# A decoder layer's cross attention: queries stacked by way of DRAM, keys in one run per row, and new orders for all engines

## What is computed

```python
x = layernorm(x + self_attn(x, W))       # one head, scores x.x/16, softmax; probabilities under 0.01 go to a rank-one term
x = layernorm(x + cross_attn(x, ctx, mask, Wq, Wk, Wv, Wo, biases))   # 16 heads of 16
x = layernorm(x + moe(x, Wr, Wi, Wo))    # 8 experts without nonlinearity, top 2 by softmax weight
```

## Time and profile before

| | us |
|---|---|
| median of 3 runs | 805.24 (804.8 to 806.78) |
| the profiled execution, its own time | 809.81 |
| its span, first to last instruction | 808.0 |
| mean granted TensorE clock | 0.979 of full speed |

### The profile page before, as it was taken

One profiled execution on the slowest core, in us unless ns is written; L12 is line 12 of the kernel. 1 busy time (PEld: TensorE's weight loads), 2 busy tenths in 40 slices (PEclk: granted clock), 3 DMA queues, 4 the chain that ended last, 5 costly groups with the idle time before them and its releaser, 6 DMA issues.

```text
span 808.0 us, 21914 instructions
## 1 busy us (share of the span) xinstructions
PE 749.3 (93%) x7176; PEld 653.1 (81%) x7176; DVE 675.4 (84%) x2563; ACT 591.1 (73%) x1447; POOL 200.8 (25%) x288
## 2 busy tenths in 40 slices
PE   5678999999999999999999999999999999999886
PEld 4557778888888878888988878888888878889764
DVE  0656778999999988999999988999999988998855
ACT  1238887787787797788777797788777797877750
POOL 2122322223212332223213332223213332231101
PEclk8979999999999999999999999999999999999988
DMA  8255554454545444554554445445544444544100
GB/s 264 67 135 138 141 134 103 122 126 128 129 122 128 115 115 119 129 127 126 130 131 121 122 112 125 127 125 130 131 126 121 118 101 130 136 113 102 43 22 26
DMA packets 95632, 96.12 MB, mean 119 GB/s; under 512 B 17808, under 2 KB 91424, under 8 KB 95520
## 3 DMA queue, kind: packets, MB, share of 16 engines
q1 hardware_dynamic: 95520, 94.73, 45.7%
HBM read 28.21 MB, written 3.67 MB: 39 GB/s over the span
## 4 chain that ended last, share of the span: by engine, by line
PE 55%; SPq 28%; DVE 8%; issue 6%; DMA 2%; ACT 1%; POOL 0%; DVEq 0%; POOLq 0%
PE psum L1387 17%; SPq L365 13%; SPq L356 10%; PE psum L1179 7%; PE psum L1210 6%; PE psum L1194 6%; PE psum L1270 3%; PE psum L1281 3%; DVE gate_p L985 3%; PE psum L1348 2%; SPq L375 2%; PE psum L1257 2%; PE psum L1314 1%; DVE scores_left L814 1%; PE psum L1292 1%
## 5 line engine op out<-in xcount | busy, mean ns | idle before, releaser
L814 DVE CUSTOM_DVE_ANT_0 scores_left<-psum,mask_add 112x375 f32<-112x375 f32 x512 | 269.5, 543 | 39.2 <-PE psum L1179 35.4
L543 ACT ACTIVATE psum<-mask_u 125x448 f32<-125x448 uint8 x384 | 207.6, 549 | 5.2
L558 ACT ACTIVATE probsT<-psum 125x448 f32<-125x448 f32 x384 | 199.6, 538 | 15.3 <-PE psum L1194 8.3
L1179 PE MATMUL psum<-k_stack,q_stack 96*112 96x376 f32 x512 | 189.6, 383 | 21.4 <-DVE nmax L814 13.9
L1194 PE MATMUL psum<-q_stack,k_stack 97*125 97x224 f32 x768 | 146.8, 287 | 6.1 <-DMA q_stack<-nmaxT 3.9
L1194 PEld LDWEIGHTS psum<-q_stack,k_stack 97*125 97x125 f32 x768 | 124.2, 188 | 15.9 <-DMA q_stack<-nmaxT 7.1
L1029 DVE SCALAR_TENSOR_TENSOR late<-psum,gate,late 128x256 f32<-128x256 f32 x224 | 107.9, 482 | 26.6 <-PE psum L1387 15.7
L1179 PEld LDWEIGHTS psum<-k_stack,q_stack 96*112 96x112 f32 x512 | 90.3, 177 | 41.4 <-DVE nmax L814 25.6
L1387 PE MATMUL psum<-we_hi,x_hi 128*128 128x512 f32 x224 | 92.1, 411 | 0.6 <-DVE gate_nmax L975 0.6
L1387 PE MATMUL psum<-we_lo,x_hi 128*128 128x512 f32 x224 | 89.7, 400 | 0.0
L1387 PE MATMUL psum<-we_hi,x_lo 128*128 128x512 f32 x224 | 89.5, 400 | 0.0
(11 more groups left out here) (158 smaller groups left out, 1625.4 us busy)
## 6 DMA issues: line engine op xcount, KB each, us to landing
k_stack<-k_hi SPq DMA_DIRECT2D x256, 93.8 KB, 2.3
q_stack<-q_hi SPq DMA_DIRECT2D x256, 56.0 KB, 2.0
ctx_sb<-in_context_T SPq DMA_DIRECT2D x32, 376.0 KB, 3.5
k_stack<-k_lo SPq DMA_DIRECT2D x128, 93.8 KB, 2.2
q_stack<-q_lo SPq DMA_DIRECT2D x128, 56.0 KB, 2.0
xT<-in_x_T SPq DMA_DIRECT2D x32, 112.0 KB, 3.1
x_sb<-in_x SPq DMA_DIRECT2D x32, 112.0 KB, 3.5
out_dram<-late SPq DMA_DIRECT2D x28, 128.0 KB, 3.1
```

Of the source, the lines that this page charges most:

```text
L543: nc.scalar.activation(psum[0:KP, ST_BANKS[i % 2], 0:4 * TOK].rearrange("p (h q) -> p h q", h=4), mask_u8[b % MASKS][:, KEYS + t * TOK:KEY ...
L558: nc.scalar.activation(probsT[:, place, i % KT, :], psum[0:KP, ST_BANKS[i % 2], 0:4 * TOK], ACT.Exp, scale=-1.0).then_inc(probs_ready, 1)
L814: nc.vector.tensor_tensor_reduce(scores_left[:, n % 2, :], psum[0:TOK, S_BANKS[n % 2], 0:KEYS], mask_add[b % 2][:, :], 1.0, 3.0e38, ALU.ad ...
L1179: nc.tensor.matmul(psum[0:TOK, S_BANKS[n % 2], 0:KEYS_EVEN], q_stack[s][0:96, c, pair, odd, :], k_stack[s][0:96, c, pair, :], start=True, ...
```

## The change

1. **Queries by way of DRAM.** `q_hi` and `q_lo` are now `[128, 2, chunk, 112]`, `q_stack` is `[97, pair, 2, chunk, 112]`. After the split the low and the high part are each written whole to a scratch tensor in DRAM (`low_queries_out`, `high_queries_out`: 128 rows of 1,792 bytes, 224 KB each), and three loads (`stack_queries`, one per third, 224 KB each) bring them into the stack, each pair's rows to the same 32 partitions. The third with the low part waits for the low store, the second third for the high store. One semaphore counts the three loads, and scores 0 waits for all of them, where pair by pair was waited for.
2. **Keys in one run.** `k_hi`, `k_lo` have 376 columns, `k_stack` is `[97, pair, chunk, 376]`; a key transfer moves 32 rows of 3,008 bytes (before: 32 x 2 runs of 1,500). The pad column is now cleared in the parts, not in the stacks. Still three transfers per pair.
3. The maxima go to row 96 in 8 pieces; the blocks read the queries as two runs of 112 columns. 
4. **New waits:** the context load waits for `ctx_lo` of two batches before; `q_hi0` no longer waits for the stacks (it follows in order behind other waits).
5. **New orders on all engines**, and iterations begin at -5; SyncE's and GpSimd's offsets count one iteration earlier for the same work. Bank order (`USES`) follows.

```diff
-        q_stacked = [[sem(f"q_stacked{k}_{pair}") for pair in range(PAIRS)] for k in range(STACKS)]
+        q_hi_out, q_lo_out = [[sem(f"{part}_out{k}") for k in range(2)] for part in ("q_hi", "q_lo")]
+        q_stacked = [sem(f"q_stacked{k}") for k in range(STACKS)]
...
             def load_context(b):
+                if b >= 2:
+                    sp.wait_ge(done["ctx_lo"], b - 1)
+                settle(sp)
...
+            def high_queries_out(b):
+                sp.dma_start(q_scratch[b % 2][0], q_hi[:, :, :, :].rearrange("p h c q -> p (h c q)").bitcast(fp32))\
+                  .then_inc(q_hi_out[b % 2], 16)
+
+            def low_queries_out(b):
+                sp.wait_ge(done["q_lo0"], b + 1)
+                settle(sp)
+                sp.dma_start(q_scratch[b % 2][1], q_lo[:, :, :, :].rearrange("p h c q -> p (h c q)").bitcast(fp32))\
+                  .then_inc(q_lo_out[b % 2], 16)
+
+            def stack_queries(b, third):
+
+                if third == 1:
+                    sp.wait_ge(q_hi_out[b % 2], turn(b, 1, 2))
                     settle(sp)
-                for third, part in enumerate((q_hi, q_hi, q_lo)):
-                    sp.dma_start(q_stack[b % STACKS][32 * third:32 * third + 32, :, n, :, :].bitcast(fp32),
-                                 part[32 * n:32 * n + 32, :, :, :].bitcast(fp32)).then_inc(q_stacked[b % STACKS][n], 16)
+                if third == 2:
+                    sp.wait_ge(q_lo_out[b % 2], turn(b, 1, 2))
+                    settle(sp)
+                sp.dma_start(q_stack[b % STACKS][32 * third:32 * third + 32, :, :, :, :]
+                             .rearrange("p n h c q -> p n (h c q)").bitcast(fp32),
+                             q_scratch[b % 2][(0, 0, 1)[third]].rearrange("(n p) x -> p n x", n=PAIRS))\
+                  .then_inc(q_stacked[b % STACKS], 16)
...
                 for third, part in enumerate((k_hi, k_lo, k_hi)):
-                    sp.dma_start(k_stack[b % STACKS][32 * third:32 * third + 32, :, n, 0:KEYS].bitcast(fp32),
-                                 part[32 * n:32 * n + 32, :, :].bitcast(fp32)).then_inc(k_stacked[b % STACKS][n], 16)
+                    sp.dma_start(k_stack[b % STACKS][32 * third:32 * third + 32, n, :, :].rearrange("p c k -> p (c k)").bitcast(fp32),
+                                 part[32 * n:32 * n + 32, :, :].rearrange("p c k -> p (c k)").bitcast(fp32)).then_inc(k_stacked[b % STACKS][n], 16)
...
                 if n < PAIRS:
-                    pe.wait_ge(q_stacked[s][n], turn(b, 3, STACKS))
+                    if n == 0:
+                        pe.wait_ge(q_stacked[s], turn(b, 3, STACKS))
                     pe.wait_ge(k_stacked[s][n], turn(b, 3, STACKS))
```

More of the change, by code:

```diff
@@ L458, in fill_ones @@
                 if k == 2:
-                    pool.wait_ge(done["x1_bo"], 3)
+                    pool.wait_ge(done["rstd1"], 3)
                 nc.gpsimd.memset(k_stack[k][96:97, :, :, :].bitcast(fp32), 1.0).then_inc(setup_pool, 1)
@@ L499, in x1_bo @@
                     pool.wait_ge(setup_dve, 8)
-                nc.gpsimd.tensor_tensor(x1_plus[b % 3][:, :], x1[b % 2][:, :], bo_row[:, :], ALU.add)\
-                  .then_inc(done["x1_bo"], 1)
+                nc.gpsimd.tensor_tensor(x1_plus[b % 3][:, :], x1[b % 2][:, :], bo_row[:, :], ALU.add)
             def mask(b):
@@ L717, in _ @@
+                at(it + 1, q_hi1)
                 at(it - 2, x2_hi)
+                at(it - 1, exponent, 8)
                 at(it + 1, q_hi0)
+                at(it + 2, sparseT)
+                at(it - 1, lay_mask, 10)
+                at(it - 1, exponent, 9)
+                at(it, v2)
+                at(it - 1, lay_mask, 11)
+                at(it, nmaxT0)
+                at(it + 2, high_context)
+                if it == 0:
+                    high_expert(5)
+                at(it - 1, exponent, 10)
@@ new lines, in _ @@
+                at(it - 1, exponent, 11)
+                if it == -2:
+                    high_expert(0)
+                at_tile(it - 2, gate_exp)
+                at(it, lay_mask, 0)
+                at(it, lay_mask, 1)
+                if it == 2:
+                    high_expert(7)
+                at(it + 1, v0)
+                at(it + 1, v1)
+                at(it - 1, o_sb)
+                at(it, exponent, 0)
+                at(it, exponent, 1)
+                at(it, lay_mask, 2)
+                at(it + 3, self_exponent)
@@ L758, in _ @@
                     nc.vector.memset(v_sb[k][:, :, :, HEAD_DIM:HEAD_DIM + 1], 1.0)
-                nc.vector.memset(k_stack[k][0:96, :, :, KEYS:KEYS_EVEN].bitcast(fp32), 0.0)
+            for part in (k_hi, k_lo):
+                nc.vector.memset(part[:, :, KEYS:KEYS_EVEN].bitcast(fp32), 0.0)
             nc.vector.memset(o_bank[:, 0:GROUPS * TOK], 0.0)
```

410 lines of the change are left out of this document (190 added, 220 removed), and 20 rows, old and new, of tables (STEPS, USES).

## The result

The changed kernel took 765.88 us (median of 4 runs, 765.52 to 766.98), the kernel before 806.01 beside it (804.8 to 809.13): ratio 0.950, 95% interval 0.947 to 0.953. The direction was forecast; the time was not: 781, with a low end of 768. The profiled execution took 766.06 us (span 764.3). The spans of the two profiles differ by 43.7 us, and about 3.6 of that is that the profiled execution of before stood above its median.

A forecast was written before the change was run, and what follows sets the result against it. TensorE was busy 93%; SyncE's queue barely kept up in full periods and fell behind in tileless ones. Full periods 11, pairs 6, first intervals 4.5 and prologue 2.5 sum to 24 us: median 805.24 to 781, range 768 to 799.

The forecast's parts named there:

- Full periods: 20 periods with a tile's four expert blocks: earlier ctx_lo shortens gate_p, removing TensorE's stall at scores 14; 0.55 us each, 11 us.
- Bounds for a full period: 0, and 23.27 - 22.66 = 0.61 us: Gain per full period limited to its 23.27 us less TensorE's busy 22.66; 0.55 taken, near the upper end.
- The Trainium skill's rule for the coincidence: VectorE and GpSimd share a port pair under exclusive lock; gate_p ends with ctx_lo; up to 0.9 us of VectorE back.
- Pairs: Three pairs of a tileless period and the next, 43.14 us each: queue relief gains 2.0 each, 6 us; bounds 0 and 3.4.
- first three intervals: First three mx1 intervals, 22 us each, about the queue's own 21: gain 4.5 us, bounds 0 and 8.1.
- 33 x 0.64 against 23.14: SyncE's 33 issues a batch take 21.1 us at most; the queue barely keeps up with a 23.14 us full period.
- k_hi0, which waits for the last key pair ... is paid in the pairs: In tileless periods queries come about 0.8 us late and k_hi0 by more, its key pair now issued behind the queries.
- Prologue: Start of the kernel: earlier weight split and 17 stack issues for 24, against the DRAM route; gain 2.5 us, bounds -4.2 and 6.1.
- The queries' route: Store and load through DRAM, 6.2 us in place of 2.0, covered by 3.4 us slack ahead of scores 0: cost nothing.
- Rival D: Slower: the DRAM route is longer than its rows and delays scores 0 of every batch; 829 us at 1.5 us late; 0.07.
- rival B: The stall moves: full periods stay at 23.2 because aT, K0 or m2 waits for VectorE; 792 us; 0.20.
- rival C: Short and early periods were held by waits within them and the longer route, not the queue; 792 us; 0.12.

The follow-up runs named there:

- e3: The changed kernel with one move undone: ScalarE's high_context put back behind gate_exp, so GpSimd's ctx_lo runs later; 793.2 us, ratio 0.977.
- e4: The kernel before with only the context copy moved early (high_context right behind nmaxT0, low_context ahead of var3 and x1_bo); 796.6 us, ratio 0.981.
- e11: The kernel before with new layouts and DRAM route, early context copy, late expert products 0 and 1, move_head ahead of the stores; 781.8 us, ratio 0.965.
- e2: The kernel before with the change's layouts and route through DRAM (26 issues), otherwise old orders; 802.7 us, ratio 0.990.
- e8: The changed kernel with three more 8 KB stores a batch behind high_queries_out (29 issues); 782.3 us, ratio 0.966.
- e9: The changed kernel with two buffers for k_hi, so k_hi0 no longer waits for the last key pair of the batch before; 762.1 us, ratio 0.940.
- e13: e8 (three more issues a batch) with e9's two buffers for k_hi; 775.3 us, ratio 0.959.
- e7: The kernel before with expert products 0 and 1 and their copies moved behind att and behind the split of the weights; 799.2 us, ratio 0.987.
- e1: The changed kernel with queries sent SBUF to SBUF again (33 issues on SyncE instead of 26), all new orders kept; 854.9 us, ratio 1.055.
- e5: As e1, but the second maxima row is issued ahead of the last three query transfers; 924.8 us, ratio 1.140.
- e14: e5 (direct queries, 33 issues) with two buffers for k_hi; VectorE's k_lo0 still waits for the last key pair; 854.0 us, ratio 1.055.

## Why the prediction was right and wrong

**Full periods (11 us forecast, 18.8 measured): the step that failed is "Bounds for a full period: 0, and 23.27 - 22.66 = 0.61 us".** I took 0.55 a period; the mean period fell by 0.94, above that bound. Busy time was taken for work. It is a union of rows that overlap and run on under a wait, so it holds part of the wait (e3: 22.54 us with the wait, 22.27 without). The cause of the stall was right and is shown from both sides (e3, e4), but it was worth 0.65 to 0.76 us in the typical period, not the 0.49 of the bracket, and 0.16 came from places without any bracket (e11 against after). By starts, in one period of each kernel: oT and the wait ahead of scores 14 took 1.09 us from start to start before and 0.35 after, the 16 scores 3.53 and 3.31, the blocks 2.91 and 2.83.

The Trainium skill's rule for the coincidence ("SBUF — State Buffer", section "SBUF: two separate sides") held: gate_p ended with ctx_lo again in e3 (1.56 us) and took 0.19 in e4. The part that the prediction thought might come back did: the mask operation now meets another small VectorE instruction, top_f, which takes 0.37 us at the median where it took 0.17. In the period shown both end within 0.02 us of each other. Of the 0.95 us that gate_p gave, VectorE loses 0.20 again there. In e4, where the copy stands in the old order, the first q_lo instruction of VectorE overlaps ctx_lo and grows from 0.42 to 0.94 us at the median, so e4's gain is net of that too. GpSimd's mask and VectorE's top_f after, and top_f's line after and before:

```profile
421.00 1.18 POOL L524 TENSOR_SCALAR mask_add<-mask_u 112x375 f32<-112x375 uint8 x1
...
421.83 0.37 DVE L1017 CAST top_f<-top_i 128x8 f32<-128x8 uint32 x1
...
L1017 DVE CAST top_f<-top_i x28: 171/373/457, 112.5 to 752.8; 128x8 f32<-128x8 uint32 x28
...
L1000 DVE CAST top_f<-top_i x28: 170/171/173, 129.5 to 796.6; 128x8 f32<-128x8 uint32 x28
```

**Pairs (6 forecast, 6.4) and first three intervals (4.5, 5.7):** right in size. The reason given was half of it. "33 x 0.64 against 23.14" treats the queue as a throughput; e2 with 26 issues in the old order gains 1.1 us a pair. e8's 29 in the new one lose 1.5 of the change's 2.1 us a pair and nearly all of its gain in the first intervals, though e8's queue still has 152 us of gaps where the kernel before had 24. What decides is what stands between the first maxima row and the key pair, the maxima row or the loads that somebody waits for. The step "k_hi0, which waits for the last key pair ... is paid in the pairs" is shown (e9, e13).

**Prologue (2.5 forecast, 8.0):** the term was mis-sized, and its upper bound of 6.1 was none. The mechanism is the one named (the split weights no longer wait behind the first product): e7 alone gives 8.5. Its K0 starts 7.3 us earlier, more than the 4.89 of the wait. TensorE still runs the same three products ahead of K0; but before, VectorE stood still for 14.45 us until product 0 could be copied, and the attention and first norm of batch 0 came behind that copy, with the split weights last. In e7 they run while product 0 still waits for its weights (that wait is 2.56 us at TensorE where it was 5.48), and the split weights are done at 16.61 instead of 29.91. VectorE's first copy before, and the last part of the split in e7:

```profile
19.91 0.69 DVE L799 TENSOR_TENSOR we_lo<-psum,we_hi 128x512 fp32r<-128x512 f32 x1 [14.45 <-ACT we_hi L688]
```

```profile
15.93 0.68 DVE L776 TENSOR_TENSOR wv_lo<-wv_sb,wv_hi 128x512 fp32r<-128x512 f32 x1
```

The route was priced at -4.2 where e2's start is 1.4 later, since its hops lie beside other work. What the lower clock gave back (last section) is in the 8.0 too.

**Tail (0 forecast, 4.7):** the sum has no term for it, so it stood at nothing without a reason. Its shape is that of the first intervals, periods with less to do; e7 gains 1.8 there, e8 loses 3.9. That it shares their cause is argued; how the 4.7 divide is open.

**The queries' route (nothing in full periods):** right; no wait for the q stack is left in them. Hops of 2.2 or 2.5 and 3.6 us at the median make 5.8 to 6.1, near the 6.2 that was taken. The long receipt of a store to DRAM, of which the prediction warned, did not show: a key transfer from SBUF to SBUF lands after 2.2 us as well, and the long part is the load. The 3.1 us against 2.0 that the prediction took as agreeing compared 128 KB with 56 KB, and loads stood at 3.1 too. Rival D fell on this, rival B on the full period of 22.31, rival C on the short periods, rival E on the total. The low end, 768, was the sum of the upper bounds; two of these weren't bounds (the full periods' and the prologue's), and the tail had none.

**Open:** which moves make the last 14 us between e11 and the changed kernel was not tried one by one, and e2's and e4's pairs hold what my own placing of move_head and low_context cost. In e1, e5 and e14 the shares of the waits for the last key pair (k_hi0, k_lo0, scores 3) and of the clock weren't taken apart by a run.

## To carry to other kernels

Take a wait's worth from the distance between starts of the same instructions with and without it, never from the idle time in brackets, and don't use an engine's busy time as the floor of a period. On a queue in order, ask of each issue what its landing releases and how many issues stand ahead of it since the last wait; the count per period says little. One landing can have several waiters: curing ScalarE's left TensorE's (e14). Cost the start and the end of a pipeline too: here they were 12.7 of 43.7 us.
